# Second-batch projections made inside the attention of a differential-attention and mixture-of-experts layer

## The reference, cut to what matters

```
x: (2, 2048, 256) f32; 16 heads, head size 16, two score maps a head
Q = x @ Wq; K = x @ Wk            # (2, 2048, 512): per head Q1|Q2, K1|K2
V = x @ Wv                        # (2, 2048, 256)
attn = softmax(Q1 K1^T / 4) - lamb * softmax(Q2 K2^T / 4)
y = layernorm(x + layernorm((attn @ V) @ Wo))
out = layernorm(y + experts(y))   # 8 experts, the best 2 for each token
```

## Time and profile before

| | us |
|---|---|
| median of 3 runs (3152.31 to 3153.23) | 3152.41 |
| the profiled execution's own time | 3153.83 |
| its span, first to last instruction | 3152.1 |
| attention's first score pair | 175.53 |

### The profile page before, as it was taken

One profiled execution on the slowest core, in us unless ns is written; L12 is line 12 of the kernel. 1 busy time (PEld: TensorE's weight loads), 2 busy tenths in 40 slices (PEclk: granted clock), 3 DMA queues, 4 the chain that ended last, 5 costly groups with the idle time before them and its releaser, 6 DMA issues. The chain is left out here.

```text
span 3152.1 us, 77474 instructions
## 1 busy us (share of the span) xinstructions
PE 2982.8 (95%) x30985; PEld 1278.8 (41%) x30986; DVE 2857.3 (91%) x3113; ACT 2582.2 (82%) x4760; POOL 588.4 (19%) x678
## 2 busy tenths in 40 slices
PE   8999999999999999999999999999999995999995
PEld 4433333333333333333333333333333274888884
DVE  3589999999999999999999999999999587777775
ACT  3259999999999999999999999999999944555554
POOL 2011101200110011011101100120111065344544
PEclk9989999999999999999999999999999996999997
DMA  6531102110220212021102112120211075222224
GB/s 158 128 61 44 35 9 49 35 35 19 62 35 15 35 42 41 13 49 35 35 9 48 45 29 35 42 35 16 39 48 58 19 264 190 36 45 44 44 45 131
DMA packets 111752, 170.10 MB, mean 54 GB/s; under 512 B 24056, under 2 KB 70896, under 8 KB 108752
## 3 DMA queue, kind: packets, MB, share of 16 engines
q1 hardware_dynamic: 97808, 146.81, 18.7%
q0 software_dynamic: 13632, 18.91, 3.8%
HBM read 97.00 MB, written 68.68 MB: 53 GB/s over the span
## 5 line engine op out<-in xcount | busy, mean ns | idle before, releaser
L1054 DVE TENSOR_REDUCE half_max<-scores 128x2 f32<-128x1024 f32 x2016 | 2295.2, 1211 | 10.3 <-PE scores L807 4.5
L978 ACT ACTIVATE probs<-bank 128x512 f32<-128x512 f32 x4012 | 2141.4, 595 | 142.6 <-PE bank L820 45.1
L879 PE MATMUL bank<-probs,V 128*32 128x256 f32 x16384 | 1309.4, 391 | 44.1 <-ACT probs L978 42.2
L807 PE MATMUL scores<-K,Q 48*128 48x512 f16 x4032 | 794.0, 388 | 2.5 <-SPq L550 2.2
L820 PE MATMUL bank<-Q,K 50*128 50x512 f16 x4012 | 790.2, 380 | 0.0
L879 PEld LDWEIGHTS bank<-probs,V 128*32 128x32 f32 x16384 | 322.6, 108 | 581.9 <-issue 516.6
L807 PEld LDWEIGHTS scores<-K,Q 48*128 48x128 f16 x4032 | 194.3, 93 | 833.2 <-DVE half_max L1054 531.0
L820 PEld LDWEIGHTS bank<-Q,K 50*128 50x128 f16 x4012 | 371.4, 94 | 184.3 <-ACT probs L978 4.2
L686 POOL TENSOR_SCALAR max_parts<-row_max 128x16 f16<-128x16 f32 x64 | 16.2, 253 | 1909.9 <-DVE row_max L1060 1909.9
L1631 PE MATMUL py<-W,hs 128*128 x1704 | 199.3, 274 | 19.3 <-issue 16.2
L1612 PE MATMUL pre<-xs,w 128*128 128x128 f16 x3408 | 205.1, 221 | 3.8 <-DVE xs L1721 3.8
(11 more groups left out here) (201 smaller groups left out, 1513.2 us busy)
## 6 DMA issues: line engine op xcount, KB each, us to landing
w_in<-in_L_ffn_w_dram SPq DMA_DIRECT2D x32, 512.0 KB, 4.6
attended<-att SPq DMA_DIRECT2D x64, 256.0 KB, 3.1
Q<-q_parts SPq DMA_DIRECT2D x96, 128.0 KB, 6.6
K<-k_parts SPq DMA_DIRECT2D x96, 128.0 KB, 7.1
values<-attended SPq DMA_DIRECT2D x6, 2048.0 KB, 10.2
q_parts<-parts SPq DMA_DIRECT2D x64, 128.0 KB, 2.4
k_parts<-parts SPq DMA_DIRECT2D x64, 128.0 KB, 2.4
w_parts<-w_out SPq DMA_DIRECT2D x16, 512.0 KB, 5.4
```

The lines of the kernel that those rows point to most:

```text
L807: mm = nc.tensor.matmul(scores[:, b, h, :], Q[p][r, c, up, t * P:(t + 1) * P], K[p][r, up, kc * TC:(kc + 1) * TC], start=True, stop=True)
L879: mm = nc.tensor.matmul(banks[att_bank[s // KB]][32 * u:32 * u + 32, q], V[wp][:, wk, u // 2, :], probs[:, 4 * s % RING + u, q], start=(wk ...
L978: nc.scalar.activation(probs[:, i % RING, :], banks[tile_bank[i]][:], ACT.Exp, scale=SCALE).then_inc(exp_done, 1)
L1054: nc.vector.tensor_reduce(half_max[lc % 2][:, :, up, t, kc], scores[:, b], AX.X, ALU.max).then_inc(max_done[b], 1)
```

## The change

The projection stage makes the first batch alone: 32 items and 16 value tiles. Eight lead items come first (Q and K of the first 128 features in all four blocks, which hold the first group), then the value tiles of blocks two to four, then the group's load, and the other 24 items with all 32 first-score pairs behind them, one or two an item, in two PSUM buffers that alternate. Four buffers hold the four column blocks. SP issues the group's loads, then ten small constants, then one 2 MB load of the second batch's columns.

The second batch's 32 items are made in the first 512 steps of the attention, in two halves of 256 tokens (steps 3 and 7 of each chunk), and its 16 value tiles at step 12 of sixteen chunks, 80 groups of two products in all. Each group stands behind the first two transposed tiles of its step on TensorE, takes the next bank of the ring, and is copied out by ScalarE behind that step's first two exponentials, item halves to SBUF and value tiles to `values`. GpSimd makes the high and the low part of an item, SP stores them, a chunk later. The loads of the second batch's groups wait for these stores. The weights, the later columns and the buffers lie in the SBUF space of `W2`, so that the splits of W1 now all come in the first four passes and those of W2 in the last four.

```diff
+    LEAD = 2 * CH
+    order = [(n, i) for n in range(CH) for i in (0, MC)]
+    order += [(n, i) for n in range(CH) for i in range(ITEMS) if i % MC > 0]
+    ALL = len(order)
+    pairs_of = {LEAD + at: range(2 * PRE * at // (ALL - LEAD), 2 * PRE * (at + 1) // (ALL - LEAD)) for at in range(ALL - LEAD)}
...
+        pv = ps("pv", [P, TPC // 2, 2, D], F32)
+        first = [ps("first_scores", [P, 2, TC], F32)[:], pv[:].rearrange("p b j d -> p b (j d)")]
...
+            for at, (n, i) in enumerate(order):
+                if at == LEAD:
+                    load_first_group()
                     for dst, src in consts:
                         sp.dma_start(dst, src).then_inc(consts_loaded, 16)
...
+                    sp.dma_start(x_later[:], x_cols.rearrange("(k p) t -> p k t", p=P)[:, :, S:2 * S]).then_inc(later_loaded, 16)
+                sp.wait_ge(lo_ready, at + 1)
...
+            for at, (n, i) in enumerate(order):
+                if at == LEAD:
+                    for v in range(1, CH):
+                        times_wv(v, range(TPC))
+                if at < LEAD and i == 0:
+                    pe.wait_ge(cols_loaded[n], 16)
+                if at >= 4:
+                    pe.wait_ge(lo_ready, at - 3)
+                for k in range(KD):
+                    mm = nc.tensor.matmul(pj[at % 4][:], wqk[:, k, i // MC, (i % MC) * P:(i % MC + 1) * P],
+                                          xT[n][:, k, :], start=(k == 0), stop=(k == KD - 1))
+                mm.then_inc(proj_ready, 1)
+                for t in pairs_of.get(at, ()):
+                    first_scores(t)
...
+            for at in range(ALL):
+                for t in pairs_of.get(at, ())[:1]:
+                    first_maximum(t)
+                low_part(at)
+                for t in pairs_of.get(at, ())[1:]:
+                    first_maximum(t)
...
+        for n in range(2 * CH * MC):
+            mc, kind, c = n // (2 * CH), n // CH % 2, n % CH
+            for half in range(2):
+                later[n * KB + (3, 7)[half]] = ("qk", n, mc, kind, c, half)
+        for v in range(KB):
+            later[(2 * v - v // 4) * KB + 12] = ("v", v)
...
+            for b in range(2):
+                for i in range(UNITS * (step + LAG) + 2 * b, UNITS * (step + LAG) + 2 * b + 2):
+                    tile_bank[i] = ring[used % 3]
+                    tile_after[i] = last.get(tile_bank[i])
+                    last[tile_bank[i]] = ("tile", i)
+                    used += 1
+                if b == 0 and step in later_at:
+                    n = later_at[step]
+                    later_bank[n] = ring[used % 3]
+                    later_after[n] = last[later_bank[n]]
+                    last[later_bank[n]] = ("later", n)
+                    used += 1
...
+            def split_later(n):
+                pool.wait_ge(later_copied, half_at[n, 1] + 1)
...
+                nc.gpsimd.tensor_copy(late_parts[:, n % 2, 0, :], late_f32[:, n % 2, :]).then_inc(later_high, 1)
...
+                nc.gpsimd.tensor_tensor(late_parts[:, n % 2, 1, :], late_f32[:, n % 2, :], late_parts[:, n % 2, 0, :],
+                                        ALU.subtract).then_inc(later_low, 1)
...
+            def project_later(step):
+                n, kind = later_at[step], later[step][0]
+                bank_free(later_after[n])
+                for k in range(KD):
+                    if kind == "qk":
+                        _, _, mc, m, c, half = later[step]
+                        lhsT = wqk[:, k, m, mc * P:(mc + 1) * P]
+                        rhs = x_later[:, k, c * TC + half * TC // 2:c * TC + (half + 1) * TC // 2]
+                    else:
+                        v = later[step][1]
+                        lhsT, rhs = x_later[:, k, v * P:(v + 1) * P], wv[:, k, :]
+                    mm = nc.tensor.matmul(banks[later_bank[n]][:, 0:D], lhsT, rhs, start=(k == 0), stop=(k == KD - 1))
+                mm.then_inc(later_ready, 1)
...
                     for u in range(2 * b, 2 * b + 2):
-                        scores_of(it * 4 * RS, j + LAG, u, it * RC + lc)
+                        scores_of(step, u)
+                    if b == 0 and step - LAG in later_at:
+                        project_later(step - LAG)
...
                     nc.scalar.activation(probs[:, i % RING, :], banks[tile_bank[i]][:], ACT.Exp,
                                          scale=SCALE).then_inc(exp_done, 1)
+                    if u == 1 and step - LAG in later_at:
+                        copy_later(step - LAG)
```

More of the change, by code:

```diff
@@ L208, in _ @@
             sp.dma_start(wv[:], Wv.rearrange("(k p) f -> p k f", p=P)).then_inc(wv_loaded, 16)
-            def row(v, n, parts=P):
-                return v.rearrange("(o d) -> o d", o=1).to_broadcast((parts, n))
-            load_cols(1)
+            for n in range(1, CH):
+                load_cols(n)
             consts = [(wo[:], Wo.rearrange("(k p) f -> p k f", p=P)), (gam[:], row(gamma, D)), (rw_rows[:], router_w),
@@ L448, in stage_attend @@
         CT = UNITS * KB
-        ring, spare = [0, 1, 2], 3
[L451 to L468, removed]
+        MC = 2 * D // P
+        later = {}
+        for n in range(2 * CH * MC):
+            mc, kind, c = n // (2 * CH), n // CH % 2, n % CH
+            for half in range(2):
+                later[n * KB + (3, 7)[half]] = ("qk", n, mc, kind, c, half)
@@ new lines, in stage_attend @@
+        for v in range(KB):
+            later[(2 * v - v // 4) * KB + 12] = ("v", v)
+        LATER = len(later)
+        later_at = {step: n for n, step in enumerate(sorted(later))}
+        half_at = {(later[step][1], later[step][5]): n for step, n in later_at.items() if later[step][0] == "qk"}
+        value_at = {later[step][1]: n for step, n in later_at.items() if later[step][0] == "v"}
+        LATE_ITEMS = 2 * CH * MC
+        assert max(later_at) < STEPS // 2 and max(value_at.values()) < later_at[(RC * (PAIRS // 2 - 1) + CH) * KB + 3]
@@ new lines, in stage_attend @@
+        ring, spare, idle_bank = [0, 1, 3], 2, 2
+        tile_bank, tile_after, later_bank, later_after, att_bank, att_after, last = {}, {}, {}, {}, [], [], {}
+        for i in range(FIRST):
+            tile_bank[i] = ring[(CT - FIRST + i) % 3]
+            tile_after[i] = last.get(tile_bank[i])
+            last[tile_bank[i]] = ("tile", i)
+        ring, spare = [0, 1, 2], 3
+        for step in range(STEPS):
+            if step % KB == 0:
+                lc, used = step // KB, 0
+                att_bank.append(spare)
+                att_after.append(last[spare])
+                if lc > 0:
+                    last[att_bank[lc - 1]] = ("attended", lc - 1)
+            for b in range(2):
+                for i in range(UNITS * (step + LAG) + 2 * b, UNITS * (step + LAG) + 2 * b + 2):
+                    tile_bank[i] = ring[used % 3]
+                    tile_after[i] = last.get(tile_bank[i])
+                    last[tile_bank[i]] = ("tile", i)
+                    used += 1
[5 more added lines that the diff above has]
+                    used += 1
+            if step % KB == KB - 1:
+                oldest = (used - 2) % 3
+                ring, spare = [ring[(oldest + 1) % 3], ring[(oldest + 2) % 3], spare], ring[oldest]
@@ L609, in _, with load_later_qk @@
+            def load_later_qk(p, g):
+                if g >= G:
+                    for i in range(2):
+                        sp.wait_ge(later_stored[i], 32 * CH * ((g - G) // 2 + 1))
+                load_qk(p, g)
             load_max(1, 0)
@@ L990, in copy_att @@
                 act.wait_ge(att_stored[lc % 2], 16 * (it * CH + lc // 2) + 1)
-                nc.scalar.copy(att[lc % 2][:], banks[att_bank[lc]][:]).then_inc(att_copied, 1)
-            for ls in range(LAG):
-                exps(0, ls)
+                nc.scalar.copy(att[lc % 2][:], banks[att_bank[it * RC + lc]][:]).then_inc(att_copied, 1)
+            for step in range(LAG):
+                exps(step)
             for it in range(PAIRS):
```

260 lines of the change are left out of this document (139 added, 121 removed).

## The result

The changed kernel takes 3179.52 us (median of 4 runs, 3178.95 to 3180.7) against 3152.82 for the kernel before in 4 runs: a ratio of 1.0082, 95% interval 1.0065 to 1.01. It is slower by 26.7 us; the forecast was +21, and 3179.5 lies in the range 3148 to 3190.

A forecast was written before the change was run, and what follows sets the result against it. TensorE was taken to set the pace in projection and attention. 80 groups at 1.07 us (0.86 + 0.11 + 0.10) add 86 us, the projection part gives back 65: +21 on 3152.4, so 3173 us, range 3148 to 3190.

The forecast's parts named there:

- The projection part: Stage ahead of the attention: without the second batch's work it gives back 65 us, between 57 and 78.
- The bare work: Attention on TensorE: 80 groups of four matmul instructions at 0.86 us each, 68.8 us, the same work as before.
- The bank: Start of each group: it waits for the exponential whose ring bank it takes, 0.11 us late, eighty times.
- The array term: Value product behind each group: turning TensorE's array costs 0 to 0.20 us, taken as 0.10.
- The turn's wait: Turn of each chunk: TensorE's 0.66 us wait stays, being time from fresh tile to exponential, not a backlog.
- The work called free: Attention: ScalarE's copies, GpSimd's operations, SP's stores and reordered weight splits add nothing to the time.
- The bare price: Rival in the attention: bank and array turn cost nothing, net +4, 3151 to 3156 us; chance 0.18.
- VectorE's pace: Rival in the attention: VectorE sets the pace and groups partly vanish into TensorE's waits, 3117 to 3145 us; chance 0.10.
- The ring: Rival in the attention: the ring stalls, each group costs about a copy more, 30 us, net +51, 3203; chance 0.08.
- A projection part bound by the group's load: Case ahead of the attention: only 57 us given back, net +29, inside the forecast's range; no chance of its own.

The follow-up runs named there:

- Experiment 1: The changed kernel with each of the 80 groups making only one of its two products: 3145.54 us, 0.9968 of the kernel before.
- experiment 2: The changed kernel with each group behind the second two transposed tiles of its step instead of the first two: 3187.06 us, 1.0098 of the kernel before.
- Experiment 6: The changed kernel with whole items at the turns of the first 32 chunks, value tiles two to a group: 3145.11 us, 0.9967 of the kernel before.
- experiment 3: The changed kernel with the same products in 40 groups, whole items and paired value tiles, instead of 80: 3169.74 us, 1.0036 of the kernel before.
- experiment 7: The changed kernel with items at turns, pairs four items later, column load in four, last four pairs behind the last item: 3135.76 us, 0.9941 of the kernel before.

## Why the prediction was right

The forecast was +21 and 26.7 were measured. By the spans the loss of 25.7 parts as follows. 68.8 us of products were moved. The attention grew by 90.1, 21.3 more than that: the price of 80 groups. The part ahead of it shrank by 63.8, 5.0 less than that, chiefly because its two waits grew by 1.6 (for K) and 3.7 (at the end). The rest lies behind the attention.

**The projection part: right, in part by luck.** The group loaded at 48.69 (47.5 said, where the terms given, 33.3 and 14, make 47.3), TensorE's wait 7.43 (6.7), the last pair at 104.58 (105.0), the restart at 110.94 (110.5, with a wait at the end of 5.97 for 5.5). It gives back 64.6 of the 65 said. Each term is near, but the closeness of the sum is luck: the group came 1.2 us later than said, and from there to the end of the last pair it took 56.3 us instead of 57.5. At the attention's first value product 63.8 are left: its first steps run at a clock of 0.50 (112 to 132), where those of before ran at 0.53 (176 to 196).

**The bare work: right.** 0.86 a group, the same in the attention as in the projection. Experiment 1 shows that TensorE pays for it in full.

**The bank: right.** 0.11 late was worked out from the exponential's end and the 0.05 behind it; the group starts 0.42 behind the tiles instead of 0.31, each time 0.05 behind an exponential's end, and experiment 2 moves this term alone.

**The array term: too small.** This is the term that was mis-sized. It was taken at 0.10, halfway between nothing and the 0.20 that a pair behind an item shows. The value product behind a group pays 0.20 as well (1.06 less 0.86), and so it is in experiments 1 to 3 at three lengths of group (0.19, 0.20, 0.20). With it the sum was 1.17 a group, 94 us and a net of +29; measured are 1.14, 90.1 and +26.7 by the medians. Of the 0.03 that is left, 0.01 is that the product starts 0.31 to 0.33 behind the tiles without a group, and not 0.31 alone; the rest stays open. There was no row for nothing at all, and one for 0.20: the row should have been taken. The Trainium skill, "TensorEngine Tiling (Array Packing)", Tiling Modes, gave the same side, that changing the tiling mode drains TensorE. The runs agree with a fixed price at each such change; whether all of the 0.20 is the drain, or part of it a first weight load that nothing covers, they don't tell apart.

**The turn's wait: right.** It stays at 0.66, since it is the time of an exponential and no backlog. Experiment 6 shows the other side: work put into that very wait costs 0.94 less an item.

**The work called free: right.** ScalarE's copy of 0.37, GpSimd's split and SP's stores put no wait on TensorE: its list of waits from 132 to 1340 us holds the turns and nothing else:

```profile
PE bank L959 <- ACT probs L1058: 19.8, 30, 0.7
```

**The rivals.** The bare price (+4) falls with experiment 3: 0.28 comes on top of each group. VectorE's pace (3117 to 3145) falls with experiment 1 and with VectorE's 0.99 of idle time at a group; the 531 us that the page put down to VectorE's maxima at the weight loads of the score pairs were no time that a group could vanish into. The ring does not stall: the half-step behind the group is 1.11 (535.85 to 536.96). A projection part bound by the group's load would give back 57; it gave 64.6.

## What to carry to other kernels

Work moved from one stage to another costs what it cost before if the same engine sets the pace in both, however idle the others are, and each place where it is put has a fixed price on top (some 0.28 us here, whether the group is 0.43 or 1.72 long): move it in few, whole pieces. Look first for a wait of that engine that is a latency and not a backlog, as the 0.66 at each turn: the same work put there cost 1.34 an item instead of 2.28, and the change became a gain. When a gap is filled, ask what the gap had kept back: here stores, which now went out right behind a 2 MB load and came back as a wait of 5.33 us ten us later.

## What the runs showed of the hardware that was not expected

- Two 128 KB stores issued 0.5 and 1.1 us behind a 2 MB load landed after 10.1 us each instead of 2.4, the first of them as the load did, and held ScalarE, VectorE and TensorE in turn. The list of TensorE's waits named only the last of them.
- The price around a full-width group between narrower tiles, 0.26 to 0.29 us, did not depend on its length over a factor of four.
- After the wait of 5.97 us at the stage's end TensorE was granted 0.50 of its clock for the next 20 us (112 to 132), and so it was after the wait of 2.77 in experiment 7 (103 to 123); after the 2.23 of the kernel before it was 0.53 (176 to 196). The shorter waits did not keep the clock up.
